# RWKV block on one core: the sum with xn moved from VectorE to accumulating DMAs for four of five mixes

## The chip, the core and the metric

The kernel runs on one core of a Trainium2 chip. Its engines are named as in the profile: PE (TensorE matmul), PEld (its weight loads), DVE (VectorE), ACT (ScalarE), POOL (GpSimd), SP (SyncE, which here only issues DMAs). The metric is the device time in microseconds of one execution, median over runs. All arithmetic is float32.

## What is computed

A batch of 64 sequences of 64 tokens, 256 channels, 32 heads of size 8, goes through one RWKV layer. Cut to what matters:

```python
xn = ln(x, ln1_w, ln1_b)
sx = token_shift(xn, state[:, i1])                 # previous token's xn minus this token's
xxx = tanh((xn + sx * maa_x) @ maa_w1)             # five low-rank heads of 32
xxx = matmul(xxx.reshape(b, l, 5, 1, 32), maa_w2)
x5 = xn[:, :, None] + sx[:, :, None] * (maa_stack + xxx)     # the five mixes
w = exp(-exp(time_decay + tanh(x5[:, :, 1] @ decay_w1) @ decay_w2))
r, k, v = x5[:, :, 3] @ Wr.T, x5[:, :, 0] @ Wk.T, x5[:, :, 2] @ Wv.T
g = silu(x5[:, :, 4] @ Wg.T)
# per head, over time: out = r . (u * k v + s);  s = k v + w * s
# group norm, gate by g, @ Wo.T, residual, second layer norm and a gated feed-forward part
```

The change concerns only how `xn` gets into `x5` (the line of the five mixes).

## The kernel before

**Tiling.** The 64 sequences are cut into nine chunks, `SEQS = [4, 6, 8, 8, 8, 8, 8, 8, 6]`; a full chunk has 512 tokens. Channels lie on the 128 partitions in two halves (`HF = 2`), tokens on the free axis, so a tile such as `sx`, `mix` or one slot of `x5` is 128 x (2 x 512) f32, that is 512 KB.

**Stages.** The work of a chunk has three parts, spread over successive turns of one software-pipelined loop. Part A: moments (`st`) and normalization (`nrm`) of x, transposition (T1), `xn`, token shift, low-rank unit W1, tanh (`th`), X0 to X4 with `mix0` to `mix4`, projections P0 (v), P1 (k), D1/D2 (decay), P3 (r), P4 (gate). Part B, in four quarters q: products k v (`a0` to `a3`, L392), scans over time (`sc0` to `sc3`, L403), products with r (`rs0` to `rs3`, L411), sums over k on PE (S0 to S3, L780). Part C: `att`, centering (`cen`), variance (VR), `gate`, output projection (WO), residual (`res`), second norm (`st2`, `rd2`, `nrm2`, T2, `xn2`), `shift2`, RR, KK, Y2, `out`.

**The order.** Every engine runs a list written out by hand (`DVE_ORDER`, `PE_ORDER`, `ACT_ORDER`, `POOL_ORDER`, `SP_ORDER`): in turn i, the stage with lag g works on chunk i - g. Engines run their lists strictly in order and meet only at semaphores. There are NCH + LAGS turns. All DMAs are issued from SP.

**Around the change.** ACT writes `xn` after T1 into `xnp`, a tile padded with one column ahead of each sequence; POOL copies the previous row of the state into that column (`a_prev`, L272). DVE forms `sx` in one subtraction over `xnp` (L328), then `mix` (L335). `a_mix` computes x5 slot <- (psum + maa) * sx in two instructions (L352), and, for all mixes but the decay one (n = 2), waits for them and adds `xnp` in a third over both halves (L360), on which the projection waits through `x5_ready`. For the decay mix PE adds the part of xn itself, with extra matmuls in `d1` (L744). x5 has three slots. The psum tensors are few: `pa` holds T1, X0, P0, P1, D1, P3, P4 in turn; `pb` holds W1, X1 to X4, D2, CB; `pc` holds part C.

**v's way.** After P0, ACT copies v into `v_sb`, SP stores it to a DRAM scratch (`vst`, L208), waits until it has landed, and loads it back broadcast over k in two halves, `vrep` (`vl0`, `vl1`, L221, 2 MB each for a full chunk); `a0` waits for the first half, and `vl1` is issued when `a3` of the chunk before is done.

**Small POOL work.** The power for the norm scales (`rd1`, `rd2`: L282, L284, L286), the initial states (`s00` to `s03`, L296) and the previous rows (L272).

Of the kernel before, what the change touches and what calls it, by code (L numbers as in the profile page):

```python
# [6 lines left out]
ALU = mybir.AluOpType  # L7
ACT = mybir.ActivationFunctionType
# [23 lines left out]

DVE_ORDER = [("rk", 2), ("out", 4), ("sc0", 2), ("cen", 3), ("bonus", 2), ("rs0", 2), ("shift", 1), ("a1", 2),
             ("gate", 3), ("sc1", 2), ("mix0", 1), ("res", 3), ("mix1", 1), ("a2", 2), ("mix2", 1), ("rs1", 2),
             ("sc2", 2), ("mix3", 1), ("rs2", 2), ("shift2", 3), ("a3", 2), ("mix4", 1), ("sc3", 2),
             ("rs3", 2), ("a0", 1), ("att", 2)]
PE_ORDER = [("M", 3), ("CB", 2), ("T1", 1), ("VR", 3), ("S0", 2), ("W1", 1), ("X0", 1), ("WO", 3), ("X1", 1),
            ("P0", 1), ("X2", 1), ("P1", 1), ("X3", 1), ("S1", 2), ("D1", 1), ("T2", 3), ("X4", 1), ("P3", 1),
            ("RR", 3), ("S2", 2), ("KK", 3), ("D2", 1), ("S3", 2), ("Y2", 3), ("P4", 1)]
ACT_ORDER = [("w", 2), ("tg", 2), ("sq", 3), ("xn", 1), ("rstd", 3), ("th", 1), ("st", 0), ("v", 1),  # L40
             ("st2", 3), ("k", 1), ("nrm2", 3), ("xn2", 3), ("thd", 1), ("nrm", 0), ("rr", 3), ("kk", 3),
             ("r", 1)]
POOL_ORDER = [("prev1", 1), ("s01", 2), ("rd1", 0), ("s02", 2), ("rd2", 3), ("s03", 2), ("s00", 1),
              ("prev2", 2)]
SP_ORDER = [("lx", 0), ("so", 4), ("lr", 3), ("vst", 1), ("vl0", 1), ("vl1", 1)]
LAGS = 4

# [9 lines left out]
def extent(c):  # L57

    return SEQS[c], SEQS[c] * L, SEQS[c] * L // P


def build(nc, x, prev, s0, vecs, w1, w2, dw1, dw2, large, consts, out):

    vscr = nc.dram_tensor("v_scratch", [2, E * T], F32, kind="Internal").ap()
    with ExitStack() as ctx:
        def sb(name, shape):
            return ctx.enter_context(nc.sbuf_tensor(name, shape, F32))

        def sem(name):
            return ctx.enter_context(nc.semaphore(name))  # L70
# [24 lines left out]
        xhat = sb("xhat", [P, TT, E])  # L95
        xnp = sb("xnp", [P, HF, NB, L + 1])
        sx = sb("sx", [P, HF, T])
        mix = sb("mix", [P, HF, T])
        th = sb("th", [P, 2, T])
        x5 = sb("x5", [P, 3, HF, T])  # L100
        v_sb = sb("v_sb", [P, JH, T])
# [39 lines left out]
        mean1_ready, var1_ready, xhat_ready, sx_ready, mix_ready = [sem(n) for n in ("mean1_ready", "var1_ready", "xhat_ready", "sx_ready", "mix_ready")]  # L141
        mixed, x5_ready, rk_ready, bonus_ready, sg_ready = [sem(n) for n in ("mixed", "x5_ready", "rk_ready", "bonus_ready", "sg_ready")]
        kv_ready, state_ready, rs_ready = [sem(n) for n in ("kv_ready", "state_ready", "rs_ready")]
# [10 lines left out]

        e_buf = sb("e_buf", [P, HF, T])

        rk, kk_buf, xhat2, sx2 = th, sq, ob, sq

# [11 lines left out]
        def x5_slot(n):  # L170
            return n % 3

        def summed_mixes(c, n):

            return 4 * c + (n + 1 if n < 2 else n)

# [85 lines left out]
        def _(pool):  # L262
# [4 lines left out]

            def put_prev(c, dst, row, done):
                if c == 0:
                    pool.wait_ge(in_prev, 16)  # L270
                nb = extent(c)[0]
                pool.tensor_copy(dst[:, :, 0:nb, 0], prev_sb[:, row, :, FIRST[c]:FIRST[c] + nb]).then_inc(done, 1)  # L272

# [25 lines left out]
            def a_prev(c):  # L299
                if c >= 1:  # L300

                    pool.wait_ge(x5_ready, 4 * c)
                    pool.wait_ge(d1_done, c)
                put_prev(c, xnp, 1, prev1_put)

            def c_prev(c):
                if c >= 1:

                    pool.wait_ge(xk_ready, c)
                put_prev(c, xn2p, 0, prev2_put)  # L310

            stages = {
                "prev1": a_prev, "prev2": c_prev,
                "rd1": lambda c: token_scale(c, mean1, var1, rs1, sh1, begun1, powered1, scale1_ready, var1_ready, xhat_ready),
# [8 lines left out]
        def _(dve):  # L323
            def a_shift(c, p):
                dve.wait_ge(xn_ready, c + 1)
                nb, n = extent(c)[0:2]
                dve.wait_ge(prev1_put, c + 1)
                dve.tensor_tensor(sx[:, :, 0:n].rearrange("p a (b t) -> p a b t", t=L),  # L328
                                  xnp[:, :, 0:nb, 0:L], xnp[:, :, 0:nb, 1:L + 1], ALU.subtract).then_inc(sx_ready, 1)
                dve.wait_ge(sx_ready, c + 1)  # L330
                if c >= 1:

                    dve.wait_ge(w1_done, c)
                for a in range(HF):
# [321 lines left out]
        def _(pe):  # L656
# [68 lines left out]
            def p_unit(c, p, n, name, freed, done):  # L725
                pe.wait_ge(x5_ready, summed_mixes(c, n))
                if c == 0 and n in (0, 3):
                    pe.wait_ge(in_vk if n == 0 else in_rg, 16)
                if freed is not None:

                    pe.wait_ge(freed, c + 1)
                project(c, pa, lambda a: weight(name, a), x5[:, x5_slot(n)], done)

            def d1(c, p):
                pe.wait_ge(mixed, 5 * c + 3)
                pe.wait_ge(k_ready, c + 1)
# [13 lines left out]
                ins.then_inc(d1_done, 1)  # L750
# [143 lines left out]
```

## Time and profile before

| | |
|---|---|
| median of three runs | 627.14 us (627.03 to 631.15) |
| span of the profiled execution | 625.9 us |
| PE / DVE / ACT / POOL busy | 77% / 85% / 41% / 13% of the span |
| chain that ended last | DVE 57%, PE 17%, issue 14%, DMA 5%, ACT 5%, POOL 1% |

The span runs from the first to the last instruction. In the 40 slices of the page DVE stands at 9 tenths or more from the sixth slice to the thirty-third; before and after that (about the first 80 us and the last 110 us) the pipeline fills and drains.

### The profile page before, as it was taken

Reading aid. Unit: us, or ns where it says so; the run is one execution under the profiler, and the core shown is the slowest. Engines: PE = TensorE matmul, PEld = TensorE weight load, DVE = VectorE, ACT = ScalarE, POOL = GpSimd, SP = SyncE. Lnnn points to the kernel's source line nnn. Section 1 sums busy time; section 2 is a strip of 40 time slices with the busy share of each in tenths; the row PEclk is TensorE's granted clock in tenths of the full one; section 3 lists DMA queues with packets and bytes.
Section 4 is the critical chain, followed back from the end, with each engine's and each line's share of the span. In section 5 each row is a group of like instructions: output and inputs, shape, how many; then the busy total and the mean of one; then the engine's idle time right before and its main releaser. Section 6 shows DMA issues by size and latency. Waiting matters only on the chain.

```text
span 625.9 us, 5759 instructions
## 1 busy us (share of the span) xinstructions
PE 482.9 (77%) x1952; PEld 268.5 (43%) x1952; DVE 530.9 (85%) x630; ACT 257.2 (41%) x529; POOL 84.2 (13%) x115
## 2 busy tenths in 40 slices
PE   2958879887978789878887988788887788538435
PEld 1734534543444336433542554344444444325223
DVE  1467899999999999999999999999999998674321
ACT  3333553543542543463445544426431532231231
POOL 1101103101200131002210122023100310020000
PEclk9979879989998999999998998999999998758669
DMA  8260911950294018600761067204820542000100
GB/s 309 73 139 26 206 46 35 201 144 0 68 212 117 2 50 183 169 2 29 165 159 51 12 157 160 68 0 123 180 67 2 126 103 67 0 2 0 59 0 25
DMA packets 19301, 55.30 MB, mean 88 GB/s; under 512 B 1096, under 2 KB 14536, under 8 KB 16712
## 3 DMA queue, kind: packets, MB, share of 16 engines
q1 hardware_dynamic: 19272, 54.94, 35.3%
q8 instruction: 15, 0.25, 0.2%
q14 instruction: 14, 0.11, 0.1%
HBM read 46.55 MB, written 8.39 MB: 88 GB/s over the span
## 4 chain that ended last, share of the span: by engine, by line
DVE 57%; PE 17%; issue 14%; DMA 5%; ACT 5%; POOL 1%; DVEq 0%; SPq 0%; POOLq 0%; ACTq 0%
DVE kv L403 19%; DVE kv L392 8%; DVE kv L411 7%; PE pc L675 7%; DVE x L352 6%; DMA vrep<-v_scratch 3%; PE pa L668 2%; DVE sx L328 2%; DMA v_scratch<-v_sb 2%; DVE trr L466 2%; DVE sq L452 2%; DVE att L432 1%; PE pb L694 1%; DVE xk L457 1%; DVE xres L446 1%
## 5 line engine op out<-in xcount | busy, mean ns | idle before, releaser
L403 DVE TENSOR_TENSOR_SCAN kv<-w_sb,kv 128x512 f32<-128x512 f32 (+2 forms) x144 | 147.3, 1084 | 0.1
L668 PE MATMUL pa<-x,large_sb 128*128 128x512 f32 (+2 forms) x288 | 121.0, 564 | 9.7 <-DVE x L360 9.1
L392 DVE TENSOR_TENSOR kv<-vrep,k_sb 128x504 f32<-128x504 f32 (+2 forms) x144 | 80.2, 619 | 6.4 <-DMA vrep<-v_scratch 6.4
L668 PEld LDWEIGHTS pa<-x,large_sb 128*128 128x128 f32 x288 | 54.6, 195 | 65.1 <-issue 43.0
L411 DVE TENSOR_TENSOR kv<-kv,r_sb 128x2048 f32<-128x2048 f32 (+2 forms) x36 | 73.8, 2049 | 0.3
L780 PE MATMUL patt<-kv,const_sb 128*32 128x512 f32 (+2 forms) x288 | 38.2, 606 | 31.8 <-DVE kv L411 31.7
L282 POOL TENSOR_SCALAR rs<-var 128x4 f32<-128x4 f32 (+2 forms) x18 | 19.4, 1075 | 311.9 <-ACT xhat L506 182.6
L352 DVE SCALAR_TENSOR_TENSOR x<-pb,vec_sb,sx 128x512 f32<-128x512 f32 (+2 forms) x72 | 46.1, 682 | 7.9 <-PE pb L717 6.5
L717 PE MATMUL pb<-th,w_sb 128*128 128x512 f32 (+2 forms) x108 | 46.6, 555 | 0.0
L296 POOL COPY kv<-s_sb 128x32 f32<-128x32 f32 (+2 forms) x36 | 17.7, 492 | 179.6 <-PE patt L780 179.6
L675 PE MATMUL pc<-large_sb,att 128*128 128x256 f32 x128 | 33.6, 420 | 10.5 <-DVE att L438 10.5
L360 DVE TENSOR_TENSOR x<-x,xnp 128x1024 f32<-128x1024 f32 (+2 forms) x36 | 39.9, 1109 | 1.2
L675 PE MATMUL pc<-large_sb,xr 128*128 128x256 f32 x128 | 34.4, 428 | 7.8 <-DVE xr L457 7.8
L675 PE MATMUL pc<-large_sb,sq 128*128 128x256 f32 x128 | 34.2, 425 | 3.2 <-ACT sq L642 3.2
L560 ACT ACTIVATE v_sb<-pa 128x1024 f32<-128x1024 f32 (+2 forms) x9 | 8.4, 929 | 68.1 <-PE pa L668 68.1
L675 PEld LDWEIGHTS pc<-large_sb,att 128*128 128x128 f32 x128 | 26.8, 214 | 20.1 <-DVE att L438 14.9
L675 PEld LDWEIGHTS pc<-large_sb,xr 128*128 128x128 f32 x128 | 27.3, 218 | 16.9 <-DVE xr L457 12.2
L675 PEld LDWEIGHTS pc<-large_sb,sq 128*128 128x128 f32 x128 | 26.5, 213 | 15.1 <-issue 6.5
L694 PE MATMUL pb<-mix,w_sb 128*128 128x512 f32 (+2 forms) x36 | 21.6, 738 | 13.2 <-DVE mix L335 13.2
L797 PE MATMUL pc<-sq,const_sb 128*128 128x512 f32 (+2 forms) x36 | 19.5, 673 | 15.8 <-ACT sq L611 15.8
L668 PE MATMUL pc<-xk,large_sb 128*128 128x512 f32 (+2 forms) x72 | 29.6, 554 | 2.5 <-ACT trr L633 2.5
L633 ACT ACTIVATE trr<-pc 128x1024 f32<-128x1024 f32 (+2 forms) x9 | 8.4, 930 | 54.5 <-PE pc L675 54.5
(81 smaller groups left out, 735.9 us busy)
## 6 DMA issues: line engine op xcount, KB each, us to landing
vrep<-v_scratch SPq DMA_DIRECT2D x12, 2048.0 KB, 12.5
vrep<-v_scratch SPq DMA_DIRECT2D x4, 1536.0 KB, 10.1
x_tok<-in_x SPq DMA_DIRECT2D x6, 512.0 KB, 13.9
v_scratch<-v_sb SPq DMA_DIRECT2D x12, 256.0 KB
xres<-in_x SPq DMA_DIRECT2D x6, 512.0 KB, 4.6
out<-ob SPq DMA_DIRECT2D x6, 512.0 KB, 3.2
vrep<-v_scratch SPq DMA_DIRECT2D x2, 1024.0 KB, 9.6
w_sb<-in_w SPq DMA_DIRECT2D x1, 1024.0 KB, 6.3
```

The lines of the kernel that those rows point to most:

```text
L282: pool.tensor_scalar(rs, var[:, 0:n], 1.0 / E, EPS, ALU.mult, ALU.add).then_inc(begun, 1)
L352: ins = dve.scalar_tensor_tensor(out=x5[:, slot, a, 0:nt], in0=src[:, a, 0:nt], scalar=vec(f"maa{g}", a), in1=sx[:, a, 0:nt], op0=ALU.add, ...
L360: dve.tensor_tensor(dst, dst, xnp[:, :, 0:nb, 1:L + 1], ALU.add).then_inc(x5_ready, 1)
L392: ins = dve.tensor_tensor(kv[:, q % 2, d, 0:nb, 1:L], vv[:, G4 * j + d, :, 0:L - 1], kk, ALU.mult)
L403: ins = dve.tensor_tensor_scan(flat, w_sb[:, p, q % HF, 0:nb].rearrange("p b t -> p (b t)"), flat, 0.0, ALU.mult, ALU.add)
L411: dve.tensor_tensor(flat, flat, r_sb[:, p, q % HF:q % HF + 1, 0:n].broadcast_to([P, G4, n]), ALU.mult).then_inc(rs_ready, 1)
L668: ins = pe.matmul(dst[:, m, 0:n], w(a)[:, m * P:(m + 1) * P], src[:, a, 0:n], start=(a == 0), stop=(a == HF - 1))
L675: ins = pe.matmul(pc_tok[:, t], src[:, a, t * P:(t + 1) * P], w(a), start=(a == 0), stop=(a == HF - 1))
L694: pe.matmul(pb[:, 0, 0:n], w1_sb[:, a, 0:P], mix[:, a, 0:n], start=(a == 0), stop=(a == HF - 1))
L717: ins = pe.matmul(dst[:, m, 0:nt], w2_sb[:, g, m * P:(m + 1) * P], th[:, 0, 0:nt], start=True, stop=True)
L780: ins = pe.matmul(patt[d * H:(d + 1) * H, j, 0:n], sum_k[:, half, :], kv[:, q % 2, d, 0:nb].rearrange("p b t -> p (b t)"), start=(half == ...
L797: ins = pe.matmul(pc[:, 1, 0:n], head_mean, sq[:, j, 0:n], start=(j == 0), stop=(j == JH - 1))
```

## The change

For the mixes n = 0, 1, 3, 4 the third DVE instruction is gone. POOL waits for `mixed` and issues a DMA with an accumulating add from `xn` into the x5 slot, SBUF to SBUF; the projection waits for its landing (`x5_added[n]`). There are four such DMAs a chunk, 36 in all, each 512 KB for a full chunk. The order of the queues changes too:

- `xn` is no longer padded. DVE subtracts only columns 1 to 63 of each sequence into `sx`; POOL computes the first column (state row minus xn) with a `tensor_tensor` that waits for `xn_ready`, and `mix` waits for it. ACT's `xn` now waits until all four accumulations of the chunk before have landed.
- x5 has four slots instead of three. To make room `e_buf` now shares the tile `mix`, so `mix` waits for `w_ready` of the chunk before.
- Turns are cut at another place (LAGS 6 instead of 4). Seen along a chunk, DVE does `shift` before `rs0`, `sc1` after `mix0`, `a2`, `mix1` and `res`, and `rk` and `att` before `a0`. PE does S0 between W1 and X0, X1 before WO, T2 ahead of S1 and X4, D1 after S2, RR before P3. ACT does `rr` and `r` before `kk`, and `xn` ahead of `sq`. SP issues the load of the next x (`lx`) between `vst` and `vl0` and not after `vl1`, and `lr` before `so`. POOL's `rd2` stands behind `ad1`, its `rd1` and `s03` behind `ad3`.

```diff
--- before.py
+++ after.py
@@ -30,20 +30,19 @@
 NQ = JH * HF
 
 
-DVE_ORDER = [("rk", 2), ("out", 4), ("sc0", 2), ("cen", 3), ("bonus", 2), ("rs0", 2), ("shift", 1), ("a1", 2),
-             ("gate", 3), ("sc1", 2), ("mix0", 1), ("res", 3), ("mix1", 1), ("a2", 2), ("mix2", 1), ("rs1", 2),
-             ("sc2", 2), ("mix3", 1), ("rs2", 2), ("shift2", 3), ("a3", 2), ("mix4", 1), ("sc3", 2),
-             ("rs3", 2), ("a0", 1), ("att", 2)]
-PE_ORDER = [("M", 3), ("CB", 2), ("T1", 1), ("VR", 3), ("S0", 2), ("W1", 1), ("X0", 1), ("WO", 3), ("X1", 1),
-            ("P0", 1), ("X2", 1), ("P1", 1), ("X3", 1), ("S1", 2), ("D1", 1), ("T2", 3), ("X4", 1), ("P3", 1),
-            ("RR", 3), ("S2", 2), ("KK", 3), ("D2", 1), ("S3", 2), ("Y2", 3), ("P4", 1)]
-ACT_ORDER = [("w", 2), ("tg", 2), ("sq", 3), ("xn", 1), ("rstd", 3), ("th", 1), ("st", 0), ("v", 1),
-             ("st2", 3), ("k", 1), ("nrm2", 3), ("xn2", 3), ("thd", 1), ("nrm", 0), ("rr", 3), ("kk", 3),
-             ("r", 1)]
-POOL_ORDER = [("prev1", 1), ("s01", 2), ("rd1", 0), ("s02", 2), ("rd2", 3), ("s03", 2), ("s00", 1),
-              ("prev2", 2)]
-SP_ORDER = [("lx", 0), ("so", 4), ("lr", 3), ("vst", 1), ("vl0", 1), ("vl1", 1)]
-LAGS = 4
+DVE_ORDER = [("bonus", 2), ("shift", 1), ("rs0", 2), ("a1", 2), ("gate", 3), ("mix0", 1), ("a2", 2),
+             ("mix1", 1), ("res", 3), ("sc1", 2), ("mix2", 1), ("rs1", 2), ("sc2", 2), ("mix3", 1), ("rs2", 2),
+             ("shift2", 3), ("a3", 2), ("mix4", 1), ("sc3", 2), ("rs3", 2), ("rk", 1), ("att", 2), ("a0", 1),
+             ("out", 3), ("sc0", 1), ("cen", 2)]
+PE_ORDER = [("T1", 1), ("VR", 3), ("W1", 1), ("S0", 2), ("X0", 1), ("X1", 1), ("WO", 3), ("X2", 1), ("P0", 1),
+            ("X3", 1), ("P1", 1), ("T2", 3), ("S1", 2), ("X4", 1), ("S2", 2), ("D1", 1), ("RR", 3), ("P3", 1),
+            ("KK", 3), ("D2", 1), ("S3", 2), ("Y2", 3), ("P4", 1), ("CB", 1), ("M", 2)]
+ACT_ORDER = [("sq", 3), ("rstd", 3), ("th", 1), ("st", 0), ("st2", 3), ("v", 1), ("nrm2", 3), ("xn2", 3),
+             ("k", 1), ("thd", 1), ("nrm", 0), ("rr", 3), ("r", 1), ("kk", 3), ("w", 1), ("tg", 1), ("xn", 0)]
+POOL_ORDER = [("prev1", 1), ("s02", 2), ("prev2", 3), ("ad0", 1), ("ad1", 1), ("rd2", 3), ("ad3", 1),
+              ("rd1", 0), ("s03", 2), ("ad4", 1), ("s00", 1), ("s01", 1)]
+SP_ORDER = [("vl1", 4), ("lr", 5), ("so", 6), ("vst", 3), ("lx", 1), ("vl0", 3)]
+LAGS = 6
 
...
@@ -93,11 +92,11 @@
         rs1 = sb("rs1", [P, TT])
         sh1 = sb("sh1", [P, TT])
         xhat = sb("xhat", [P, TT, E])
-        xnp = sb("xnp", [P, HF, NB, L + 1])
+        xn = sb("xn", [P, HF, T])
         sx = sb("sx", [P, HF, T])
         mix = sb("mix", [P, HF, T])
         th = sb("th", [P, 2, T])
-        x5 = sb("x5", [P, 3, HF, T])
+        x5 = sb("x5", [P, 4, HF, T])
         v_sb = sb("v_sb", [P, JH, T])
         k_sb = sb("k_sb", [P, 2, HF, T])
         r_sb = sb("r_sb", [P, 2, HF, T])
...
...
@@ -265,11 +259,11 @@
             pool.memset(neg_half[:, :], -0.5).then_inc(inited, 1)
             pool.wait_ge(inited, 3)
 
-            def put_prev(c, dst, row, done):
-                if c == 0:
-                    pool.wait_ge(in_prev, 16)
-                nb = extent(c)[0]
-                pool.tensor_copy(dst[:, :, 0:nb, 0], prev_sb[:, row, :, FIRST[c]:FIRST[c] + nb]).then_inc(done, 1)
+            def add_xn(c, n):
+
+                pool.wait_ge(mixed, 5 * c + n + 1)
+                nt = extent(c)[1]
+                pool.dma_start(x5[:, x5_slot(n), :, 0:nt], xn[:, :, 0:nt], accum_op=ALU.add).then_inc(x5_added[n], 16)
 
...
@@ -297,20 +291,25 @@
                                  s0_sb[:, half, G4 * j:G4 * (j + 1), FIRST[c]:FIRST[c] + nb]).then_inc(s0_put, 1)
 
             def a_prev(c):
-                if c >= 1:
-
-                    pool.wait_ge(x5_ready, 4 * c)
-                    pool.wait_ge(d1_done, c)
-                put_prev(c, xnp, 1, prev1_put)
+                if c == 0:
+                    pool.wait_ge(in_prev, 16)
+                else:
+
+                    pool.wait_ge(mixed, 5 * c)
+                pool.wait_ge(xn_ready, c + 1)
+                nb, n = extent(c)[0:2]
+                first = [ap[:, :, 0:n].rearrange("p a (b t) -> p a b t", t=L)[:, :, :, 0] for ap in (sx, xn)]
+                pool.tensor_tensor(first[0], prev_sb[:, 1, :, FIRST[c]:FIRST[c] + nb], first[1], ALU.subtract).then_inc(prev1_put, 1)
 
             def c_prev(c):
                 if c >= 1:
 
                     pool.wait_ge(xk_ready, c)
-                put_prev(c, xn2p, 0, prev2_put)
+                nb = extent(c)[0]
+                pool.tensor_copy(xn2p[:, :, 0:nb, 0], prev_sb[:, 0, :, FIRST[c]:FIRST[c] + nb]).then_inc(prev2_put, 1)
 
             stages = {
-                "prev1": a_prev, "prev2": c_prev,
+                "prev1": a_prev, "prev2": c_prev, **{f"ad{n}": (lambda c, n=n: add_xn(c, n)) for n in x5_added},
...
@@ -323,41 +322,36 @@
         def _(dve):
             def a_shift(c, p):
                 dve.wait_ge(xn_ready, c + 1)
-                nb, n = extent(c)[0:2]
+                n = extent(c)[1]
+                seqs = [ap[:, :, 0:n].rearrange("p a (b t) -> p a b t", t=L) for ap in (sx, xn)]
+                dve.tensor_tensor(seqs[0][:, :, :, 1:L], seqs[1][:, :, :, 0:L - 1], seqs[1][:, :, :, 1:L], ALU.subtract).then_inc(sx_ready, 1)
+                dve.wait_ge(sx_ready, c + 1)
                 dve.wait_ge(prev1_put, c + 1)
-                dve.tensor_tensor(sx[:, :, 0:n].rearrange("p a (b t) -> p a b t", t=L),
-                                  xnp[:, :, 0:nb, 0:L], xnp[:, :, 0:nb, 1:L + 1], ALU.subtract).then_inc(sx_ready, 1)
-                dve.wait_ge(sx_ready, c + 1)
                 if c >= 1:
 
                     dve.wait_ge(w1_done, c)
-                for a in range(HF):
-                    ins = dve.scalar_tensor_tensor(out=by_seq(mix[:, a, 0:n]), in0=by_seq(sx[:, a, 0:n]), scalar=vec("maa_x", a),
-                                                   in1=xnp[:, a, 0:nb, 1:L + 1], op0=ALU.mult, op1=ALU.add)
+                    dve.wait_ge(w_ready, c)
+                for a in range(HF):
+                    ins = dve.scalar_tensor_tensor(out=mix[:, a, 0:n], in0=sx[:, a, 0:n], scalar=vec("maa_x", a),
+                                                   in1=xn[:, a, 0:n], op0=ALU.mult, op1=ALU.add)
                 ins.then_inc(mix_ready, 1)
 
             def a_mix(c, p, n):
 
                 g = MIXES[n]
-                nb, nt = extent(c)[0:2]
+                nt = extent(c)[1]
                 src = pa if n == 0 else pb
                 dve.wait_ge(x_done, 5 * c + n + 1)
 
-                if n >= 3:
-                    dve.wait_ge([pv_done, pk_done][n - 3], c + 1)
+                if n == 4:
+                    dve.wait_ge(pv_done, c + 1)
                 elif c >= 1:
-                    dve.wait_ge([pr_done, pg_done, d1_done][n], c)
+                    dve.wait_ge([pg_done, pk_done, d1_done, pr_done][n], c)
                 slot = x5_slot(n)
                 for a in range(HF):
                     ins = dve.scalar_tensor_tensor(out=x5[:, slot, a, 0:nt], in0=src[:, a, 0:nt], scalar=vec(f"maa{g}", a),
                                                    in1=sx[:, a, 0:nt], op0=ALU.add, op1=ALU.mult)
                 ins.then_inc(mixed, 1)
-                if g == MIX_W:
-
-                    return
-                dve.wait_ge(mixed, 5 * c + n + 1)
-                dst = x5[:, slot, :, 0:nt].rearrange("p a (b t) -> p a b t", t=L)
-                dve.tensor_tensor(dst, dst, xnp[:, :, 0:nb, 1:L + 1], ALU.add).then_inc(x5_ready, 1)
 
             def a_rk(c, p):
                 dve.wait_ge(r_ready, c + 1)
...
@@ -538,9 +525,15 @@
                 act.wait_ge(t1_done, c + 1)
                 if c >= 1:
 
-                    act.wait_ge(x5_ready, 4 * c)
+                    for added in x5_added.values():
+                        act.wait_ge(added, 16 * c)
+                    act.wait_ge(prev1_put, c)
+                    act.wait_ge(mix_ready, c)
                     act.wait_ge(d1_done, c)
-                normed(c, pa, xnp, "ln1_w", "ln1_b", xn_ready)
+                n = extent(c)[1]
+                for a in range(HF):
+                    ins = act.activation(xn[:, a, 0:n], pa[:, a, 0:n], ACT.Identity, bias=vec("ln1_b", a), scale=vec("ln1_w", a))
+                ins.then_inc(xn_ready, 1)
 
             def a_tanh(c, p):
                 act.wait_ge(w1_done, c + 1)
...
@@ -723,7 +720,7 @@
                 ins.then_inc(x_done, 1)
 
             def p_unit(c, p, n, name, freed, done):
-                pe.wait_ge(x5_ready, summed_mixes(c, n))
+                pe.wait_ge(x5_added[n], 16 * (c + 1))
...
@@ -737,12 +734,12 @@
                 if c == 0:
                     pe.wait_ge(in_dw, 32)
                 n = extent(c)[1]
-                nf, bf = n // DFOLD, extent(c)[0] // DFOLD
+                nf = n // DFOLD
 
                 for a in range(HF):
                     for f in range(DFOLD):
                         pe.matmul(pa[f * DECAY:(f + 1) * DECAY, 0, 0:nf], dw1_sb[:, a, :],
-                                  xnp[:, a, f * bf:(f + 1) * bf, 1:L + 1], start=(a == 0), stop=False)
+                                  xn[:, a, f * nf:(f + 1) * nf], start=(a == 0), stop=False)
                 for a in range(HF):
                     for f in range(DFOLD):
                         ins = pe.matmul(pa[f * DECAY:(f + 1) * DECAY, 0, 0:nf], dw1_sb[:, a, :],
```

## Rows read from the trace of the kernel before

**Rows 1.** The page: its head line and part 1.
```profile
span 625.9 us, 5759 instructions
PE 482.9 (77%) x1952; PEld 268.5 (43%) x1952; DVE 530.9 (85%) x630; ACT 257.2 (41%) x529; POOL 84.2 (13%) x115
```

**Rows 2.** Engines by stretch, one period: length, busy times, PE clock, DMA share, GB/s.
```profile
257.53:323.05 65.52, 55.06 (x226) 29.32 (x225) 65.21 (x71) 30.69 (x63) 10.96 (x12) 1.00 0.40 96
```

**Rows 3.** Groups of instructions, line 360: busy us, mean ns, idle before.
```profile
L360 DVE TENSOR_TENSOR x<-x,xnp 128x1024 f32<-128x1024 f32 (+2 forms) x36 | 39.9, 1109 | 1.2
```

**Rows 4.** Timeline of DVE, a period: start us, us, line, operation.
```profile
266.89 1.22 DVE L378 TENSOR_TENSOR bonus<-v_sb,pb 128x1024 f32<-128x1024 f32 x1
...
277.96 4.57 DVE L403 TENSOR_TENSOR_SCAN kv<-w_sb,kv 128x512 f32<-128x512 f32 x4
282.44 1.39 DVE L352 SCALAR_TENSOR_TENSOR x<-pa,vec_sb,sx 128x512 f32<-128x512 f32 x2
...
285.00 1.21 DVE L446 TENSOR_TENSOR xres<-xres,pc 128x1024 f32<-128x1024 f32 x1
...
291.09 1.40 DVE L352 SCALAR_TENSOR_TENSOR x<-pb,vec_sb,sx 128x512 f32<-128x512 f32 x2
292.41 2.28 DVE L411 TENSOR_TENSOR kv<-kv,r_sb 128x2048 f32<-128x2048 f32 x1
...
299.09 1.38 DVE L352 SCALAR_TENSOR_TENSOR x<-pb,vec_sb,sx 128x512 f32<-128x512 f32 x2
...
319.53 2.47 DVE L392 TENSOR_TENSOR kv<-vrep,k_sb 128x504 f32<-128x504 f32 x4
...
332.41 1.21 DVE L378 TENSOR_TENSOR bonus<-v_sb,pb 128x1024 f32<-128x1024 f32 x1
```

**Rows 5.** Timeline of PE in the same period.
```profile
285.14 3.70 PE L668 MATMUL pa<-x,large_sb 128*128 128x512 f32 x8 [1.60 <-DVE x L360]
...
296.63 1.08 PE L744 MATMUL pa<-xnp,dw_sb 128*64 128x256 f32 x8
297.55 1.03 PE L748 MATMUL pa<-x,dw_sb 128*64 128x256 f32 x8
...
301.15 1.95 PE L721 MATMUL pb<-th,w_sb 128*128 128x128 f32 x16
...
319.66 1.06 PE L780 MATMUL patt<-kv,const_sb 128*32 128x512 f32 x8 [2.72 <-DVE kv L411]
```

**Rows 6.** POOL's line 282: duration ns min/median/max over 18 instructions.
```profile
L282 POOL TENSOR_SCALAR rs<-var x18: 194/882/2397, 7.1 to 599.6; 128x4 f32<-128x4 f32 x12, 128x3 f32<-128x3 f32 x4, 128x2 f32<-128x2 f32 x2
```

**Rows 7.** DMA issues: count, KB each, median us from issue to landing.
```profile
vrep<-v_scratch SPq DMA_DIRECT2D x12, 2048.0 KB, 12.5
...
x_tok<-in_x SPq DMA_DIRECT2D x6, 512.0 KB, 13.9
...
xres<-in_x SPq DMA_DIRECT2D x6, 512.0 KB, 4.6
out<-ob SPq DMA_DIRECT2D x6, 512.0 KB, 3.2
```

**Rows 8.** Timeline of SP's queue: the two vrep loads (first start, last end).
```profile
299.34 11.45 SPq L221 DMA_DIRECT2D vrep<-v_scratch  x2
```

**Rows 9.** Engines by stretch, inside a vrep load: the last two are DMA.
```profile
304.00:308.00 4.00, 4.00 (x13) 2.24 (x12) 3.96 (x6) 1.02 (x3) 0.00 (x0) 1.00 1.16 246
```

**Rows 10.** Timeline of DVE while the pipeline fills.
```profile
35.65 1.42 DVE L392 TENSOR_TENSOR kv<-vrep,k_sb 128x252 f32<-128x252 f32 x4 [4.53 <-DMA vrep<-v_scratch]
...
73.52 1.94 DVE L392 TENSOR_TENSOR kv<-vrep,k_sb 128x378 f32<-128x378 f32 x4 [1.90 <-DMA vrep<-v_scratch]
...
81.03 0.94 DVE L378 TENSOR_TENSOR bonus<-v_sb,pb 128x768 f32<-128x768 f32 x1
...
124.52 2.47 DVE L392 TENSOR_TENSOR kv<-vrep,k_sb 128x504 f32<-128x504 f32 x4
...
135.75 1.22 DVE L378 TENSOR_TENSOR bonus<-v_sb,pb 128x1024 f32<-128x1024 f32 x1
```

More of the change, by code:

```diff
@@ L141, in build @@
         mean1_ready, var1_ready, xhat_ready, sx_ready, mix_ready = [sem(n) for n in ("mean1_ready", "var1_ready", "xhat_ready", "sx_ready", "mix_ready")]
-        mixed, x5_ready, rk_ready, bonus_ready, sg_ready = [sem(n) for n in ("mixed", "x5_ready", "rk_ready", "bonus_ready", "sg_ready")]
+        mixed, rk_ready, bonus_ready, sg_ready = [sem(n) for n in ("mixed", "rk_ready", "bonus_ready", "sg_ready")]
+        x5_added = {n: sem(f"x5_added{n}") for n in (0, 1, 3, 4)}
         kv_ready, state_ready, rs_ready = [sem(n) for n in ("kv_ready", "state_ready", "rs_ready")]
@@ L153, in build @@
             sem(n) for n in ("summed", "mean_done", "var_done", "wo_done", "t2_done", "rr_done", "kk_done", "y2_done")]
-        e_buf = sb("e_buf", [P, HF, T])
-        rk, kk_buf, xhat2, sx2 = th, sq, ob, sq
+        rk, kk_buf, xhat2, sx2, e_buf = th, sq, ob, sq, mix
         def vec(name, half):
@@ L170, in x5_slot @@
         def x5_slot(n):
-            return n % 3
-        def summed_mixes(c, n):
-            return 4 * c + (n + 1 if n < 2 else n)
+            return n % 4
         block = ctx.enter_context(nc.Block())
@@ L487, in _ @@
         def _(act):
-            def normed(c, src, dst, w, b, done):
-                nb, n = extent(c)[0:2]
-                for a in range(HF):
-                    ins = act.activation(dst[:, a, 0:nb, 1:L + 1], by_seq(src[:, a, 0:n]), ACT.Identity,
-                                         bias=vec(b, a), scale=vec(w, a))
-                ins.then_inc(done, 1)
             def moments(c, src, mean, var, scratch, mean_ready, var_ready, used):
@@ L625, in c_xn @@
                     act.wait_ge(xk_ready, c)
-                normed(c, pc, xn2p, "ln2_w", "ln2_b", xn2_ready)
+                nb, n = extent(c)[0:2]
+                for a in range(HF):
+                    ins = act.activation(xn2p[:, a, 0:nb, 1:L + 1], by_seq(pc[:, a, 0:n]), ACT.Identity,
+                                         bias=vec("ln2_b", a), scale=vec("ln2_w", a))
+                ins.then_inc(xn2_ready, 1)
             def c_rr(c, p):
```

## The prediction

> **What bounds the kernel now.** First the page's part 1 [rows 1]: DVE is busy 530.9 of 625.9 us, PE 482.9. A share over the whole span mixes filling, running full and draining, so next one full period by stretch [rows 2]: 65.21 of 65.52 us are DVE's, 55.06 PE's. In the full part DVE never stops, and anything taken off it shortens the period until PE, which has 10.5 us of room, or a transfer takes over. The group of the adds [rows 3] gives what can be had: 36 adds, 39.9 us. Then the timelines of the period show what is ready when [rows 4, 5], SP's queue and the table of issues what a transfer costs [rows 7, 8], and DVE's timeline while the pipeline fills [rows 10] where DVE waits today: `a0` of chunks 0 and 1 waits 4.53 and 1.90 us for `vrep`. I count time within a period from the start of `bonus` (266.89); the next one starts at 332.41, 65.52 later [rows 4].
>
> **What goes.** A mix with its add takes 285.00 - 282.44 = 2.56 us of DVE, the mix without one 292.41 - 291.09 = 1.32 [rows 4]. Each add is worth 1.24, four 4.96: DVE's own period becomes 60.56. Subtracting 63 columns in place of 64, and unpadded operands, I cost at nothing.
>
> **What comes: L, the time from the end of a mix to the landing of its accumulation.** No row shows an accumulating DMA, nor one issued by POOL. Below it is bounded by the plain 512 KB store, 3.2 us, above by a 512 KB load queued behind the two `vrep` loads, 13.9 [rows 7]. Nearest is the plain 512 KB load, 4.6 [rows 7]; the accumulation reads another 512 KB, and at the 246 GB/s of a busy stretch [rows 9] that is 2.1 more. I take L = 6.7 for a full chunk, POOL's issue within it (POOL's short instructions take 0.2 to 2.4 us [rows 6]), 5.7 for a chunk of six sequences, 4.5 for one of four.
>
> The same from the Trainium skill: "DMA: Bandwidth & Descriptors" (Anatomy of one DMA) gives 2.0 us plus bytes over 436 GB/s for a DMA issued from GpSimd, and "Collectives: The Full Stack" (The bandwidth ceiling) has an adding DMA at half the rate because it reads two sources. Estimated from these two pages, L is 2.0 + 2 x 1.2 = 4.4, and the sum below would be about 7 us lower. No row of before bears on either.
>
> **Where L lies, in a full period.** `mix0` started at 282.44 - 266.89 = 15.55, behind `sc1` of 282.44 - 277.96 = 4.48 [rows 4]. With `sc1` moved behind it, it runs from 11.1 to 12.4, so P0 can start at 12.4 + 6.7 = 19.1; it started at 285.14 - 266.89 = 18.25 [rows 5]. P0 is 0.85 late: most of L is paid by moving the scan. `mix3` started at 32.2; two adds fewer, it ends at 299.09 - 266.89 - 2.5 + 1.3 = 31.0, and X4 waits for it. Ahead of X4 PE does P0, X3, P1, T2, S1: 3.7 + 1.95 + 3.7 + 1.06 + 1.06 = 11.5, by the rows of P0, X4 and S3 [rows 5]. Only when P0 starts after 31.0 - 11.5 = 19.5, that is L over about 7.2, does L move X4. `ad1`, `ad3` and `ad4` have more room: between `mix3` and P3 PE does X4, S2, D1 and RR (some 8.4 us), between `mix4` and P4 lie over 10.
>
> **Who limits the shorter period.** From X4 to the end of S3 PE took 320.72 - 301.15 = 19.57, of which 2.72 is a wait; D1 (298.58 - 296.63 = 1.95) now lies inside: 18.8 [rows 5]. S3 ends at 31.0 + 18.8 = 49.8. DVE wants it for `att` at 319.53 - 266.89 - 4.96 = 47.7, plus 1.3 for `rk`, which now comes first: 49.0. A stall of 0.8.
> The first column of `sx` is now computed by POOL after `xn`, not copied ahead of time. It runs beside DVE's subtraction of 1.2 us, but takes 0.2 to 2.4 [rows 6], so `mix` waits 0 to 1.3; and `xn` itself now follows M, T1. I take 1.0 for both. What queues behind `mix` on DVE is all else, so it counts in full.
> Period: 60.56 + 0.8 + 1.0 = 62.4, a gain of 3.1, not 4.96.
>
> **`vrep`.** Its first load was issued at 299.34 - 266.89 = 32.45 [rows 8]. P0 is 0.85 later, so 33.3, and it lands 12.5 later [rows 7], at 45.8. The DMA engines are full during it (share 1.16 [rows 9]), and `ad3` (from 31.0) and `ad4` (from 41) now fall there: 1 MB read each, 4.3 us at 246 GB/s, so 0 to 8.6 us. Part of `ad3` precedes the load, and `ad4` shares: I take 3, landing at 48.8. `a0` is due at 49.0 + 0.8 + 1.1 = 50.9. Hidden, with 2 us to spare. The load of the next x moves ahead of `vrep` to a stretch where v's store is landing; costed at nothing, covered by that spare time. `rd1` and `s03` behind `ad3` on POOL, and SP's `lr` before `so`, have tens of us or whole quarters of slack: nothing. The fourth slot frees `mix3` and `mix4` from waits that before did not bind: nothing.
>
> **Filling.** Here L is not hidden. `a0` of chunk 0 already waited for `vrep` [rows 10], whose way starts at P0: L 4.5 for an add of about 1, so 3.5 late. Up to `shift` of chunk 1 about 1.5 is won back by less DVE work in between; 2.0 is carried. `a0` of chunk 1 (73.52) waits again: 2.0 + (5.7 - 1.0) + 1 for the crowded DMA engines = 7.7 late, 81.2. `att` and `rk`, some 1.6 for these small chunks, now lie inside the wait, so `bonus` (81.03) comes at 87.1. For `a0` of chunk 2 the load takes 48.8 less 2.5 for the smaller work ahead of `mix0` = 46.3 after `bonus`; DVE would be there at 43.5 - 4.96 + 2.2 = 40.7. So 133.4 for 124.52 [rows 10], 8.9 late, and `bonus` of chunk 2 (135.75) is 8.9 - 2.2 = 6.7 late.
>
> **Sum,** against the profile's span: +6.7 once filled; chunks 3 to 7, five periods at -3.1: -15.5; chunk 8, with three quarters of the tokens: 3.7 - 1.8 = -1.9. The draining has no mixes and keeps its order of work: 0. Together -10.7: 625.9 - 10.7 = 615.2. The median of the runs lies 1.2 above the span: **616 us**.
> Sensitivity: 3 us per us of L (the three filling chunks), 9 per us beyond L = 7.2 (six periods more). Break-even with 627 is L = 8.2: 616.4 + 1.5 + 9 x 1.0.
>
> **Rivals.**
> *The accumulation is slow.* Place: P0 waiting for `x5_added0`, then X4 and S3 late, `att` after them. It decides from L = 8.2. For it: the upper bound of 13.9, and that nothing in the trace shows the rate of an adding DMA. Against: `ad0` is issued when the engines are idle. At L = 10: 616.4 + 1.5 + 9 x 2.8 = 643, slower.
> *`vrep` becomes the wait.* With the whole 8.6 us the first load lands at 54.4, `a0` stalls 3.5 in each of six periods: 637. With two thirds of it, 1 us or less each: 620.
> *POOL is held up by DVE.* A POOL instruction of four columns takes from 0.19 to 2.40 us, median 0.88 [rows 6], while DVE is never idle: it waits out DVE instructions of up to 2.28 us [rows 4]. If issuing a DMA waits likewise once, L = 9.0: 616.4 + 1.5 + 9 x 1.8 = 634; if not always, about 627. The Trainium skill, "SBUF — State Buffer" (SBUF: two separate sides; Who interferes with whom), says that DMAs issued from GpSimd starve while DVE holds the shared ports in its two-port modes, but that an instruction with two SBUF inputs blocks only GpSimd's reads. By the second half the issue would be spared here; the stretched row agrees with the blocking of reads.
> *The whole DVE time comes back.* 24 adds at 1.24 and 8 at about 0.95 once DVE is full: 37, so 590. It needs the filling not to slip, against the waits of [rows 10].
>
> **From these the numbers.** Forecast 0.58 (own range 606, at L = 3.2, to 624); whole gain 0.06; `vrep` 0.08; POOL held up 0.08; slow accumulation 0.20. Range 602 to 643: it leaves out the whole gain and half of the slow case. A measurement here tells about 1%, 621 to 633, from no change. Faster: the whole gain and 0.49 of the forecast, 0.55. Within 1%: 0.09 of the forecast and half of `vrep` and POOL, 0.17. Slower: 0.28.
>
> **What would show it.** DVE 491 us busy; periods of `bonus` near 62.4 with gaps ahead of `mix` (POOL) and `att` (PE); `a0` of chunks 0, 1, 2 waiting for `vrep`, `bonus` of chunk 2 near 142; P0 about 6.7 after its `mix0`. Wrong would make it: P0 waiting more than 8 us after `mix0`, `a0` waiting for `vrep` in full periods, or POOL busy for several us at each `ad`.

## Result and profile after

The changed kernel takes 673.95 us (673.64 to 677.53) against 627.42 for the kernel before: ratio 1.0732, 95% interval 1.0689 to 1.0775. It is slower by 46.5 us; the forecast was 616 us. The profiled execution's span is 675.6 us.

The page, head line, part 1, and the two groups that answer to the removed adds and to the projections that wait for them:

```profile
span 675.6 us, 5784 instructions
PE 501.4 (74%) x1952; PEld 279.1 (41%) x1952; DVE 493.1 (73%) x594; ACT 258.3 (38%) x529; POOL 146.6 (22%) x151
...
L665 PE MATMUL pa<-x,large_sb 128*128 128x512 f32 (+2 forms) x288 | 141.0, 642 | 64.8 <-DMA x<-xn 64.8
...
L266 POOL DMA_DIRECT2D x<-xn x36 | 36.5, 1013 | 127.6 <-DVE x L352 127.6
```

The projections in the kernel before, from its page:

```profile
L668 PE MATMUL pa<-x,large_sb 128*128 128x512 f32 (+2 forms) x288 | 121.0, 564 | 9.7 <-DVE x L360 9.1
```

DVE has lost 37.8 us of work; the adds that went took 39.9 [rows 1, 3]. The span grew by 49.7: DVE idles more, and the projections, which cost 121.0 us of PE before, cost 141.0 and are preceded by 64.8 us of waiting for accumulations. The longest waits by name (engine, line, waited for: total, times, longest):

```profile
PE pa L665 <- DMA x<-xn: 64.8, 15, 9.9
...
DVE att L419 <- PE pc L787: 46.0, 7, 10.7
```

A full period on the timelines (start, length, engine, line, and idle before with its releaser), first PE's:

```profile
353.12 3.61 PE L665 MATMUL pa<-x,large_sb 128*128 128x512 f32 x8
...
362.82 3.72 PE L672 MATMUL pc<-large_sb,sq 128*128 128x256 f32 x16
372.17 6.65 PE L665 MATMUL pa<-x,large_sb 128*128 128x512 f32 x8 [5.63 <-DMA x<-xn]
378.66 1.88 PE L766 MATMUL pb<-th,const_sb 128*128 128x512 f32 x4
380.38 1.88 PE L787 MATMUL pc<-att,const_sb 128*128 128x512 f32 x4
```

DVE's:

```profile
313.15 1.22 DVE L372 TENSOR_TENSOR bonus<-v_sb,pb 128x1024 f32<-128x1024 f32 x1
...
368.97 4.57 DVE L397 TENSOR_TENSOR_SCAN kv<-w_sb,kv 128x512 f32<-128x512 f32 x4
382.29 1.22 DVE L419 TENSOR_TENSOR att<-att,pc 128x1024 f32<-128x1024 f32 x1 [8.75 <-PE pc L787]
383.43 1.21 DVE L372 TENSOR_TENSOR bonus<-v_sb,pb 128x1024 f32<-128x1024 f32 x1
```

The issues of SP's queue and POOL's:

```profile
345.52 7.98 SPq L215 DMA_DIRECT2D vrep<-v_scratch  x2
```

```profile
354.54 0.93 POOL L266 DMA_DIRECT2D x<-xn  x1 [1.52 <-DVE x L352]
```

`ad4` is issued at 354.54, when both `vrep` loads have been issued and neither has landed. P4 (372.17) waits for it, though PE was ready 5.6 us earlier. CB, M and DVE's `cen` (L419) stand behind P4, so DVE idles 8.75 us and the period is 383.43 - 313.15 = 70.3 us against 65.52 [rows 4]. The next four answers are durations from issue to landing: of this `ad4`, of the first load (issued at 345.5), of the second (352.9), and of the four accumulations of the period:

```profile
DMA to landing us min/median/max: 17.6/17.6/17.6
...
DMA to landing us min/median/max: 15.5/15.5/15.5
...
DMA to landing us min/median/max: 19.0/19.0/19.0
...
DMA to landing us min/median/max: 4.5/6.4/17.6
```

`ad0` and `ad1` land 4.5 us after issue, `ad3` 8.3, `ad4` 17.6: at 372.1, about when the second load lands (352.9 + 19.0 = 371.9; the first landed at 345.5 + 15.5 = 361.0). The count of packets by queue shows what happened in between. q1 carries SP's DMAs; q0, which the kernel before does not have, carries POOL's. In order, the stretches 354.54 to 361.2, 361.2 to 369, and (q0 alone) 361.2 to 372.2; each line gives packets, MB, and the share of the 16 DMA engines:

```profile
q1 hardware_dynamic: 104, 1.44, 100.7%
...
q1 hardware_dynamic: 87, 1.43, 76.3%
q0 software_dynamic: 91, 0.37, 23.9%
...
q0 software_dynamic: 144, 0.52, 24.1%
```

Until the first load has landed, not one packet of `ad4` moves; then its packets and those of the second load go through about one for one (91 and 87), and both end together.

The wait has a second price. The stretch in the middle of P4 shows the granted clock (the last three numbers are PE clock, DMA share, GB/s):

```profile
373.00:377.00 4.00, 4.00 (x6) 1.69 (x5) 0.54 (x1) 0.00 (x0) 0.00 (x0) 0.50 0.35 124
```

After 5.6 idle microseconds PE runs at 0.50 of its clock, the lower of its two levels (1.2 GHz), and P4 takes 6.65 us where P3 took 3.61. The two, 5.6 and 3.0, make up nearly all of the 8.75 that DVE waits.

Filling shows the same on a larger scale: `bonus` of chunk 2 starts at

```profile
174.55 1.21 DVE L372 TENSOR_TENSOR bonus<-v_sb,pb 128x1024 f32<-128x1024 f32 x1
```

against 135.75 [rows 10], 38.8 us late. From there to the end both kernels need 490.2 (before) and 501.0 us: 39 of the 50 us are lost before `bonus` of chunk 2, 11 after it.

The 11 us are not spread evenly. The full periods that start with `bonus` of chunks 2, 3 and 4 are 3.6 to 4.8 us longer than before. The one that ends with `bonus` of chunk 7 takes 523.30 - 449.14 = 74.16 us, 8.6 more than in the kernel before, and there it is `ad3` that is late:

```profile
449.14 1.21 DVE L372 TENSOR_TENSOR bonus<-v_sb,pb 128x1024 f32<-128x1024 f32 x1
...
499.13 6.32 PE L665 MATMUL pa<-x,large_sb 128*128 128x512 f32 x8 [9.87 <-DMA x<-xn]
...
523.30 1.22 DVE L372 TENSOR_TENSOR bonus<-v_sb,pb 128x1024 f32<-128x1024 f32 x1
```

This `ad3` was issued at 480.72, within 0.1 us of the first load, and lands 18.4 us later; in the period above it was issued 0.8 us ahead of the load and took 8.3. In this turn SP has no next x to load ahead of `vrep`, which is the visible difference; that it is the reason was not tested.

### The profile page after: what moved, and what is told of

It is laid out like the page before. It is cut to its first block, busy times and chain, and to the rows that moved or that the text cites. A ratio compares the mean times of both kernels' runs of the same rounds, so it can differ in the third digit from the quotient of the medians.

```text
span 675.6 us, 5784 instructions
## 1 busy us (share of the span) xinstructions
PE 501.4 (74%) x1952; PEld 279.1 (41%) x1952; DVE 493.1 (73%) x594; ACT 258.3 (38%) x529; POOL 146.6 (22%) x151
## 4 chain that ended last, share of the span: by engine, by line
PE 27%; DMA 24%; DVE 19%; issue 12%; POOL 9%; ACT 8%; DVEq 0%; POOLq 0%; ACTq 0%
DMA x<-xn 23%; PE pa L665 9%; DVE kv L386 5%; PE pc L672 5%; DVE x L352 4%; POOL rs L278 2%; POOL sh L280 2%; POOL rs L276 2%; PE pc L665 2%; PE pb L766 2%; DVE kv L405 2%; ACT ob L493 2%; PE pc L787 2%; ACT ob L489 2%; DVE kv L397 2%
## 5 line engine op out<-in xcount | busy, mean ns | idle before, releaser
L665 PE MATMUL pa<-x,large_sb 128*128 128x512 f32 (+2 forms) x288 | 141.0, 642 | 64.8 <-DMA x<-xn 64.8
L665 PEld LDWEIGHTS pa<-x,large_sb 128*128 128x128 f32 x288 | 64.1, 229 | 130.8 <-DMA x<-xn 72.7
L714 PE MATMUL pb<-th,w_sb 128*128 128x512 f32 (+2 forms) x108 | 51.4, 603 | 20.2 <-DVE x L352 20.2
L290 POOL COPY kv<-s_sb 128x32 f32<-128x32 f32 (+2 forms) x36 | 34.2, 964 | 138.9 <-PE patt L777 138.9
L266 POOL DMA_DIRECT2D x<-xn x36 | 36.5, 1013 | 127.6 <-DVE x L352 127.6
L419 DVE TENSOR_TENSOR att<-att,pc 128x1024 f32<-128x1024 f32 (+2 forms) x9 | 9.9, 1099 | 46.0 <-PE pc L787 46.0
L302 POOL TENSOR_TENSOR sx<-prev_sb,xn 128x16 f32<-128x16 f32 (+2 forms) x9 | 9.0, 996 | 154.0 <-ACT xn L535 154.0
L599 ACT ACTIVATE sg<-pa 128x1024 f32<-128x1024 f32 (+2 forms) x9 | 8.4, 929 | 83.0 <-PE pa L665 83.0
L714 PEld LDWEIGHTS pb<-th,w_sb 128*128 128x128 f32 x108 | 21.4, 210 | 44.9 <-DVE x L352 29.8
L489 ACT ACTIVATE ob<-xres 128x256 f32<-128x256 f32 x32 | 12.9, 404 | 60.3 <-DVE xres L440 60.3
```

What stands on the lines that cost most here:

```text
L266: pool.dma_start(x5[:, x5_slot(n), :, 0:nt], xn[:, :, 0:nt], accum_op=ALU.add).then_inc(x5_added[n], 16)
L290: pool.tensor_copy(kv[:, q % 2, :, 0:nb, 0], s0_sb[:, half, G4 * j:G4 * (j + 1), FIRST[c]:FIRST[c] + nb]).then_inc(s0_put, 1)
L489: ins = act.activation(scratch[:, t, :], src[:, t, :], ACT.Copy, scale=-1.0 / E, accum_out=mean[:, t:t + 1])
L665: ins = pe.matmul(dst[:, m, 0:n], w(a)[:, m * P:(m + 1) * P], src[:, a, 0:n], start=(a == 0), stop=(a == HF - 1))
L714: ins = pe.matmul(dst[:, m, 0:nt], w2_sb[:, g, m * P:(m + 1) * P], th[:, 0, 0:nt], start=True, stop=True)
```

## Experiments

Theory A: `ad4` cannot land beside the `vrep` loads, and P4, CB, M and `cen` wait. Theory B: the new orders cost the time. Theory C: each accumulating DMA costs alike.

**e1: the fifth mix added by VectorE**

```diff
+                if n in (4,):
+                    dve.wait_ge(mixed, 5 * c + n + 1)
+                    dve.tensor_tensor(x5[:, slot, :, 0:nt], x5[:, slot, :, 0:nt], xn[:, :, 0:nt], ALU.add).then_inc(x5_added[n], 1)
...
-              ("rd1", 0), ("s03", 2), ("ad4", 1), ("s00", 1), ("s01", 1)]
+              ("rd1", 0), ("s03", 2), ("s00", 1), ("s01", 1)]
```

> The changed kernel with one edit: the add for the fifth mix (n = 4) is done by VectorE again, the other three by accumulating DMAs. Theory A (the accumulation ad4 falls into the stretch of the two vrep loads, lands 17.6 us after its issue, and P4 waits for it; so do CB, M and cen behind it): nearly all of the wait of 5.6 us before P4 and of cen's 8 to 9 us goes; periods of 62 to 63 us instead of 69 to 70, and 625 to 640 us in all, because while the pipeline fills ad4 is the longest of the four as well. Theory B (the new order of the queues costs the time, whoever adds): within 10 us of the changed kernel, 665 to 675. Theory C (each accumulating DMA costs alike, by POOL's issue and latency): a quarter of the loss returns, about 662.

620.26 us, ratio to before 0.9861 (0.9836 to 0.9885). Taking away one DMA of four returned 54 us, more than A said, so C falls, and B with it: these are the new orders. The late `ad3` of chunk 7 is still there: the period that ends with its `bonus` takes 74.0 us, the three full ones ahead of it 61.8 to 63.3.

**e2: all four adds on VectorE,** the same edit for n in 0, 1, 3, 4, and no accumulation in POOL's list.

> The changed kernel (its orders, four slots, unpadded xn, column 0 by POOL) with all four adds on VectorE, no accumulating DMA. Theory A: the orders are near neutral in full periods, so DVE bounds again at about 65.5 plus one stall of 1 to 2; 625 to 640 us, the excess over 627 coming from the filling. Theory B: 660 to 675. Theory C: 627 to 635.

626.68 us, ratio 0.9978 (0.995 to 1.0007): the orders, the fourth slot and column 0 on POOL together change nothing that can be measured. But they do so by a loss and a gain. `bonus` of chunk 2 starts at

```profile
144.17 1.21 DVE L377 TENSOR_TENSOR bonus<-v_sb,pb 128x1024 f32<-128x1024 f32 x1
```

8.4 us later than before [rows 10], and the rest of its span of 626.9 takes 482.7 in place of 490.2.

**e3: the old orders with the DMAs**

```diff
-DVE_ORDER, PE_ORDER, ACT_ORDER, SP_ORDER, LAGS = (as changed)
+DVE_ORDER, PE_ORDER, ACT_ORDER, SP_ORDER, LAGS = (as before)
+POOL_ORDER = [("prev1", 1), ("s01", 2), ("rd1", 0), ("ad0", 1), ("ad1", 1), ("s02", 2), ("rd2", 3),
+              ("ad3", 1), ("s03", 2), ("ad4", 1), ("s00", 1), ("prev2", 2)]
```

> The changed kernel with the orders of the kernel before (LAGS 4; the four accumulations put into POOL's list behind rd1, rd1, s02's predecessor and rd2), so the DMAs without the new orders. Theory A: ad4 still shares the time with the vrep loads and lands late; P0 now waits the whole latency, since sc1 stands before mix0 again; 660 to 690 us. Theory B: near 620, since the orders were the loss. Theory C: 655 to 665.

768.6 us, ratio 1.2225 (1.2149 to 1.2301), worse than any of the three expected. PE's timeline has two kinds of wait in each period, here at P3 for `ad3` and at P0 of the next period for `ad0`:

```profile
326.44 6.38 PE L666 MATMUL pa<-x,large_sb 128*128 128x512 f32 x8 [10.58 <-DMA x<-xn]
...
377.42 6.48 PE L666 MATMUL pa<-x,large_sb 128*128 128x512 f32 x8 [5.21 <-DMA x<-xn]
```

Both are followed by a projection that takes 6.4 us in place of 3.6. With P3 ahead of RR nothing covers `ad3`, and it too now meets a load: issued at 314.05, behind the first load's 312.41, it lands at 326.4, about 1.6 us after that load, which took 12.4 us.

**e4: the second load held until `ad4` has landed**

```diff
+                if half == 1:
+                    sp.wait_ge(x5_added[4], 16 * (c + 1))
```

> The changed kernel with one wait more on SyncE: the second vrep load of a chunk is issued only after ad4 of that chunk has landed. Theory A: ad4 then shares only with the first load, lands 6 to 10 us after its issue in full periods, P4 waits for nothing, and the second load still comes in time for a1; periods of 62 to 64, total 635 to 650 (the filling gains less). Theory B: 665 to 680. Theory C: unchanged at 672 to 680.

616.93 us, ratio 0.9812 (0.9787 to 0.9837). One wait more on SP is worth 57 us, and A's expectation was too cautious. A full period is 329.82 - 268.41 = 61.41 us, read from the starts of two `bonus`; by stretch:

```profile
268.41:329.82 61.41, 55.29 (x224) 29.44 (x224) 60.47 (x67) 30.84 (x64) 19.96 (x16) 1.00 0.62 137
```

DVE is busy 60.47 of it, at the 60.56 that was worked out for it. `ad4` of this period lands 9.0 us after its issue at 309.8, at 318.8; the first load, the only one in flight, had landed at 300.8 + 15.7 = 316.5. Filling is better as well: `bonus` of chunk 2 at 148.71. The other full periods take 58.5 to 63.3 us, but the one that ends with `bonus` of chunk 7 takes 70.05: there `ad3` meets the first load, which is not held, and P3 waits 6.1 us for it.

**e5: `ad4` of half the size**

```diff
+                hs = 1 if n == 4 else HF
-                pool.dma_start(x5[:, x5_slot(n), :, 0:nt], xn[:, :, 0:nt], accum_op=ALU.add)
+                pool.dma_start(x5[:, x5_slot(n), 0:hs, 0:nt], xn[:, 0:hs, 0:nt], accum_op=ALU.add)
```

and VectorE adds the other half of the channels.

> The changed kernel, but of the last mix (n = 4) only half of the channels is added by DMA (256 KB), the other half by VectorE (0.6 us). Theory A1 (ad4 waits behind the vrep bytes because the two streams take turns and ad4's own packets get a small share): its time from issue to landing goes down with its size, from 17.6 to about 9 to 11 us, P4 no longer waits, 625 to 640 us. Theory A2 (ad4 is not served until the vrep loads that were queued before are done, whatever its size): still 15 us or more, total 665 to 675.

656.7 us, ratio 1.0448 (1.0417 to 1.0478). In a full period the 256 KB issued at 337.6 take

```profile
DMA to landing us min/median/max: 17.0/17.0/17.0
```

and land at 354.6; the second load, from 336.0 with 18.4 us, at 354.4. Half the bytes gain 0.6 us of 17.6, as A2 said. But half the bytes are not half the packets. From the issue to 344.4, when the first load lands, POOL's queue moves none; from there to 354.7:

```profile
q0 software_dynamic: 144, 0.26, 13.9%
```

These are 144 packets, as many as the whole `ad4` of the changed kernel has (0.52 MB there). So in a full period the landing fits the number of packets, taken in turn with those of the second load, and the run does not rule out the turns of A1, only its share by bytes. The total is better than A2 said (656.7, not 665 to 675), mostly by the filling (`bonus` of chunk 2 at 158.79, not 174.55). There size did count: in chunk 1 the half `ad4` lands 12.3 us after its issue, the whole one of the changed kernel 18.1.

**e9: `ad4` as a plain copy**

```diff
+                if n == 4:
+                    pool.dma_start(x5[:, x5_slot(n), :, 0:nt], xn[:, :, 0:nt]).then_inc(x5_added[n], 16)
+                    return
```

> The changed kernel, but ad4 is a plain copy of xn into the slot instead of an accumulation, issued by GpSimd at the same place (so the part sx * (maa + xxx) of the gate's mix is left out of the computation). It tells whether ad4's 17.6 us belong to accumulating or to a transfer of GpSimd's queue beside the vrep loads. If a copy is served alongside the loads: it lands in 5 to 9 us, P4 doesn't wait, 625 to 640 us. If every transfer of that queue has to let the vrep loads by: 15 to 18 us as with the accumulation, total 665 to 675.

660.4 us (two executions; ratio 1.0514, 1.0458 to 1.057). The copy of a full period and P4 behind it:

```profile
DMA to landing us min/median/max: 17.7/17.7/17.7
...
355.67 6.52 PE L668 MATMUL pa<-x,large_sb 128*128 128x512 f32 x8 [5.75 <-DMA x<-xn]
```

So in a full period neither the second read nor the adding is what takes long. While filling it is otherwise: the copy of chunk 1 lands after 9.6 us, the accumulation after 18.1, and `bonus` of chunk 2 comes at 157.92. The Trainium skill, "DMA: Bandwidth & Descriptors" (Queues, rings and completion order), has each DMA engine take turns between queues packet by packet, a packet being a run of some 9 to 17 descriptors. The trace agrees that the queues take turns in the second part of the wait: 91 packets of `ad4`, by the trace's own count, beside 87 of the second load. In the 6.7 us before that, no packet of `ad4` moved, though it had been issued. That the engines first drained a whole run of the first load would fit this part, but not the turns of one for one behind it, and no run here separates the two. What holds `ad4` back in the first part was not found out.

**e6: the held load, and chunks 0 and 1 added by VectorE.** From chunk 2 on the held load of e4; for `c < 2` VectorE does the adds of all four mixes, as e1 did for one.

> The changed kernel with the second vrep load held until ad4 has landed, and for chunks 0 and 1 the adds on VectorE instead of by DMA. Theory A with the filling priced as latency: chunks 0 and 1 lose the landing times, bonus of chunk 2 comes 4 to 5 us earlier than with the gate alone (148.7), and the total falls from 617 to 610 to 613. If the filling's delay comes from the new orders alone, no change: 615 to 618.

611.04 us, ratio 0.9729 (0.9704 to 0.9754): as expected, and the fastest version found, faster than both kernels. `bonus` of chunk 2 at 144.22, 4.5 earlier than in e4 and where e2 has it: 4.5 us is what the DMAs cost while filling, once the second load is held.

**e7: only chunks 0, 1 and 2 added by VectorE,** no held load.

> The changed kernel without the held load; for chunks 0, 1 and 2 the adds are on VectorE, from chunk 3 on by DMA. It splits the loss of 47 us between filling and full periods. Theory A: bonus of chunk 2 comes at about 144 instead of 174.6, the full periods stay at 69 to 70: 640 to 652 us. If the full periods carried most of the loss, 665 or more; if the filling carried all, 627 or less.

644.2 us, ratio 1.0236 (1.0182 to 1.0289). `bonus` of chunk 2 at 144.05 instead of 174.55; the rest of its span of 643.8 takes 499.8, the changed kernel's 501.0. The split is confirmed: 30 us of the loss are DMAs while filling, the full periods stay as long.

**e8: the old orders, `ad0` and `ad1` by DMA, the other two on VectorE**

> The orders of the kernel before, with ad0 and ad1 by DMA (they fall into a stretch without vrep loads) and the adds of n = 3 and 4 on VectorE. Theory A: P0 now waits for ad0 in every period, 4.6 us plus issue against an add of 1.1, since sc1 stands ahead of mix0; X1 and WO cover only part, so 630 to 645. If the latency of ad0 was hidden in these orders too, 612 to 620 and the new orders weren't needed.

679.82 us, ratio 1.0799 (1.0738 to 1.086), outside what I expected. No accumulation is late here (4.6 us, all away from the loads), and yet:

```profile
320.12 3.70 PE L671 MATMUL pa<-x,large_sb 128*128 128x512 f32 x8 [3.60 <-DMA x<-xn]
...
325.57 1.41 DVE L355 SCALAR_TENSOR_TENSOR x<-pb,vec_sb,sx 128x512 f32<-128x512 f32 x2 [5.21 <-PE pb L720]
```

In these orders X2 stands behind P0 on PE, and so `mix2` on DVE behind `ad0`'s landing: 5.2 us here, 7.8 in the next period. A latency of 4.6 us, uncovered, costs more than four adds of DVE.

## Why the prediction was wrong

**What held.** DVE's busy time, 491 forecast, 493.1 measured. The full period without the late `ad4`, 62.4 forecast, 61.4 in the one of e4 that is shown (58.5 to 63.3 in four of its five, 70.05 in the last); its stalls: `mix` waits 0.2 us (1.0 forecast for `xn` and column 0), `att` 0.6 (0.8). The cover of `ad0` by `sc1` moved behind it: P0 waits for nothing in full periods, and e8 shows the price without that cover.

**What failed: the step "`ad1`, `ad3` and `ad4` have more room".** I gave all four accumulations one L, 6.7, from loads that ran alone, and compared it with the 10 us between `mix4` and P4. In the paragraph on `vrep` I had `ad4` and the loads in the same stretch, but asked only how much the accumulations delay the loads (3 us; the first load's 12.5 became 15.5, but e4's took 15.7, and in the changed kernel no packet of `ad4` moved before it had landed), never how much the loads delay the accumulation. The row for that was in the list: the 512 KB load behind two `vrep` loads took 13.9 [rows 7]. It stood there as an upper bound and went into the slow rival as a property of all accumulations, not of the one that is issued at that time. With L = 17.6 for `ad4` alone against some 12 us between its issue and P4's turn, the wait is the 5.6 us of the profile, 8.75 with the clock. At the 4.5 of `ad0` everything would have been covered, which is what the estimate from the Trainium skill's two pages (4.4) gave and `ad0` and `ad1` confirm. e1 and e4 settle it from both sides: take away the transfer, or the second load beside it, and 54 to 57 us are gone. `ad3` failed by the same step in one period only, that of chunk 7.

**The filling.** Forecast was 6.7 us late at `bonus` of chunk 2, measured 38.8. By the runs: 8.4 from the orders alone (e2), 4.5 from the DMAs with the second load held (e4 against e2 and e6), 25.8 from accumulations beside both loads (the changed kernel against e4). The first term had been counted as a small gain. In e2 `rk`, now ahead of `a0`, waits 2.48 us for r in chunk 0, and `a0` still waits 4.28 for `vrep` behind it (before, 4.53 for `vrep` alone [rows 10]). The third is the failed step again: in chunk 0 of the changed kernel `rk` waits 7.58 us for r, and `bonus` 6.56 for CB behind P4.

**The sum, term by term,** forecast and measured in the changed kernel: filling +6.7 and +38.8; the five periods -15.5 and +19.3; chunk 8 -1.9 and -4.2; draining 0 and -4.2 (e2, with no DMA, has -3.2 there, so most of that is the orders). In e4 the four are +13.0, -15.0, -4.5 and -4.2: its span of 615.2 is the forecast's to the tenth, by errors that cancel, so that agreement is luck.

**The clock** was not in the sum. Each wait of over 5 us ahead of a projection in the rows shown was followed by that projection at 6.3 to 6.7 us, about 3 more than at the full clock; the wait of 3.6 us in e8 was not (3.70). Not all cost as much: in the period before the one shown P4 took 5.27 us after a wait of 5.83.

**The rivals.** *POOL held up by DVE*: not seen; POOL's issue takes 0.93 us (median), and `ad0` lands in 4.5 with DVE busy throughout. *`vrep` becomes the wait*: small, the products k v waited 2.7 us for it in all. *The whole DVE time comes back*: not seen, also not in e4, whose period is 61.4 and not 60.56. *Slow accumulation*, with 0.20, had the direction right and the place wrong: it named P0 waiting for `ad0`, then X4, S3 and `att`. P0 waits for nothing in full periods; it was P4, CB, M and `cen`. Its break-even, an L of 8.2 for `ad0`, no run tested.

## What to carry to other kernels

A transfer's time is that of the moment at which it is issued: list what is in flight then on any queue, and use the row of a transfer that met the same traffic, not that of one alone. Count packets as well as bytes. Where a large load has slack and a small transfer has none, hold the load with a wait; here that turned +7.3% into -1.9%, and keeping DMAs out of the filling made it -2.7%. An add moved to a DMA is worth its time on the full engine only where other work covers the landing, and the order must be made for that.

## What was not expected of the hardware

A 512 KB transfer from GpSimd's queue lands in 4.5 us when it is alone. Issued with both 2 MB loads of SyncE's queue in flight, it takes 16 to 20 us; with half the bytes 17.0, as a plain copy 17.7. In the full periods it landed within 0.5 us of the second load, and in e4, with one load in flight, 2.3 us after it. In the period shown the trace has two parts: no packet of it until the first load has landed, then turns of about one packet each with the second load, though a packet of `ad4` carries about 4 KB (2 in e5) and one of the load 16. It is no fixed rule that it lands with a load: in chunk 2 `ad4` landed 3.2 us ahead of the second load, and `ad3` of chunk 7 landed 5.0 us after the first.
